# Two attention layers and two feed-forward layers on one core: general path at the end, semaphores cleared as ranges, linear stage with halves in three banks

## The reference

```
x = layernorm(x + linear_attention(x))     # 16 heads of 8: elu(q)+1, elu(k)+1, running sums over time
x = layernorm(x + switch_attention(x))     # 8 heads of 64, 5 experts, 3 chosen per token and head, softmax
x = layernorm(x + rotary_attention(x))     # 16 heads of 8, rotary positions, softmax
x = layernorm(x + ffn(x))                  # only the tokens whose router weight is above the median
```

```
s_t = s_(t-1) + k_t v_t^T ;  z_t = z_(t-1) + k_t
value_t = (q_t^T s_t) / (q_t^T z_t + 1e-6)
```

## Time and profile before

| | us |
|---|---|
| median of three executions | 2010.35 |
| profiled execution, its own time | 2014.0 |
| its span, first to last instruction | 2012.1 |
| linear stage, from the start to the next stage's first instruction | 232.64 |
| expert stage, likewise | 1101.69 |
| rotary stage, likewise | 583.12 |
| depth stage, to the end of the span | 94.65 |

### The profile page before, as it was taken

How to read it: one execution, slowest core, us unless ns; L and a number is a source line. 1 busy time by engine, 2 the same in 40 slices (tenths; PEclk the granted TensorE clock), 3 DMA queues, 4 the chain that set the end, 5 groups by cost and what they waited for, 6 DMA issues and landing times. The chain is left out here.

```text
span 2012.1 us, 25633 instructions
## 1 busy us (share of the span) xinstructions
PE 1750.1 (87%) x8916; PEld 836.6 (42%) x8916; DVE 1149.1 (57%) x1834; ACT 1280.4 (64%) x2456; POOL 953.7 (47%) x565
## 2 busy tenths in 40 slices
PE   7888459999999999999999999636989999998587
PEld 3433245445555455554545544212333333332255
DVE  6988596986668876678766564240303214120267
ACT  1211205766776668766786676606999999999434
POOL 4566306778876788767888678700000000000023
PEclk9988689999999999999999999777999999999879
DMA  2000000000000000000000000013220302110001
GB/s 70 0 1 0 24 20 11 20 21 11 21 20 11 20 11 20 11 20 11 21 20 11 20 11 1 0 44 135 70 80 22 126 22 84 65 41 22 0 15 43
DMA packets 27869, 59.11 MB, mean 29 GB/s; under 512 B 3840, under 2 KB 14800, under 8 KB 27728
## 3 DMA queue, kind: packets, MB, share of 16 engines
q1 hardware_dynamic: 27728, 57.32, 8.9%
HBM read 38.44 MB, written 18.87 MB: 28 GB/s over the span
## 5 line engine op out<-in xcount | busy, mean ns | idle before, releaser
L707 POOL TENSOR_TENSOR b_psum<-b_psum,b_probs 128x1024 f32<-128x1024 f32 x192 | 460.6, 2399 | 173.8 <-ACT b_probs L847 167.1
L2020 ACT ACTIVATE c_probs<-banks 128x1024 f32<-128x1024 f32 x512 | 483.0, 1029 | 67.3 <-PE banks L2072 56.1
L1225 DVE TENSOR_TENSOR b_gated<-banks,b_g 128x480 f32<-128x480 f32 x512 | 314.2, 655 | 229.1 <-PE banks L949 224.2
L847 ACT ACTIVATE b_probs<-banks 128x1024 f32<-128x1024 f32 x256 | 254.1, 1019 | 218.5 <-PE banks L982 217.7
L949 PE MATMUL banks<-b_w,b_xh 128*128 128x480 f32 x1024 | 353.3, 399 | 33.5 <-DVE b_gated L1225 19.4
L1233 DVE TENSOR_REDUCE b_tok<-b_gated 128x192 f32<-128x960 f32 x256 | 281.4, 1138 | 0.5
L982 PE MATMUL banks<-b_qq,b_kk 64*128 64x512 f32 x1024 | 263.7, 625 | 14.7 <-DVE b_gated L1225 10.0
L818 ACT ACTIVATE b_share<-b_o,b_picked 128x64 f32<-128x64 f32 x1080 | 268.6, 338 | 0.0
L1014 PE MATMUL banks<-b_probs,b_tok 128*64 128x512 f32 x1024 | 253.5, 616 | 2.4 <-ACT b_probs L847 2.4
L2087 PE MATMUL banks<-c_probs,c_vg 128*32 128x512 f32 x2048 | 247.7, 601 | 0.3 <-DVE c_acc L2182 0.2
L949 PEld LDWEIGHTS banks<-b_w,b_xh 128*128 128x128 f32 x1024 | 195.0, 190 | 116.5 <-issue 40.3
(11 more groups left out here) (232 smaller groups left out, 1907.6 us busy)
## 6 DMA issues: line engine op xcount, KB each, us to landing
b_raw_w<-in_L_ffn_W SPq DMA_DIRECT2D x32, 480.0 KB, 3.3
c_heads<-c_split SPq DMA_DIRECT2D x24, 512.0 KB
c_keys<-c_heads SPq DMA_DIRECT2D x16, 512.0 KB, 3.7
c_queries<-c_heads SPq DMA_DIRECT2D x16, 512.0 KB, 4.6
c_heads<-c_split SPq DMA_DIRECT2D x8, 384.0 KB
a_xs<-in_L_attn_x SPq DMA_DIRECT2D x4, 512.0 KB, 7.8
out<-d_yo SPq DMA_DIRECT2D x3, 512.0 KB, 3.2
c_heads<-c_split SPq DMA_DIRECT2D x8, 128.0 KB
```

Source lines behind the costliest of these rows:

```text
L707: nc.gpsimd.tensor_tensor(psum[:, par, :], prev, probs[:, i % 4, :], ALU.add).then_inc(psum_rdy, 1)
L847: nc.scalar.activation(probs[:, i % 4, :], score_b[i % 2], ACT.Exp).then_inc(exp_rdy, 1)
L1225: nc.vector.tensor_tensor(shape(gated[:, t % 2, j, :]), shape(proj_b[u % WAYS][:, 0:HALF_W]), g.unsqueeze(2).broadcast_to([P, 3, HD2, E]), ...
L2020: nc.scalar.activation(probs[:, step % 4, c, :, :], unit_b[u % NU], ACT.Exp, scale=float(HD) ** -0.5).then_inc(exp_rdy, 1)
```

## The change

The general paths of the two attention stages, and now also a general copy of the depth stage, stand together in one block at the end (`redo_all`). It reads r1 again, so the fast rotary stage writes into a new buffer, r3, and the depth stage reads it. The two flags are kept apart and joined by a maximum; each engine loads and tests the result once. The expert stage raises its flag ahead of its last norm, and the rotary stage counts and raises its flag ahead of and between its last pieces.

Semaphores are kept in a `Signals` object per stage. They are cleared by GpSimd at the start of the next stage's block, one instruction per run of adjacent numbers, so a stage is followed by one barrier and no clearing block. The depth stage's weights are loaded at the end of the rotary stage's SP program.

In the linear stage a column of v is made and multiplied by k in halves of 512 time steps, in three single banks in rotation. The fourth bank's first element holds the constant 1 that the scan reads, broadcast. `scan` and `qscan` have three buffers.

The diff, cut to its core (re-indented lines of the stages are left out):

```diff
+    def clear(self, eng):
+        numbers = sorted(handle.num for handle in self.handles)
+        first = 0
+        for n in range(1, len(numbers) + 1):
+            if n == len(numbers) or numbers[n] != numbers[n - 1] + 1:
+                eng.sem_clear(range(numbers[first], numbers[n - 1] + 1))
+                first = n
...
 def only_if(eng, flag):
-    return nullcontext() if flag is None else eng.If(eng.value_load(flag[0:1, 0:1], min_val=0, max_val=1))
+    return eng.If(eng.value_load(flag[0:1, 2:3], min_val=0, max_val=1))
...
-def linear_scans(nc, x_dram, out, ps, ident, I):
+def linear_thirds(nc, x_dram, out, ps, ident, I, place, signals):
...
-        ones = sb("ones", [P, T])
-        kv, scan, qscan = sb("kv", [P, 3, T]), sb("scan", [P, 2, T]), sb("qscan", [P, 2, T])
+        kv, scan, qscan = sb("kv", [P, 3, T]), sb("scan", [P, 3, T]), sb("qscan", [P, 3, T])
-        v_b, num_b = [bank2(0), bank2(2)], bank2(4)
+        v_b, one, num_b = [ps[:, i, :] for i in range(3)], ps[:, 3, 0:1], bank2(4)
...
-            nc.gpsimd.memset(ones[:, :], 1.0).then_inc(ones_rdy, 1)
...
-                if j == 2:
+                if j == 3:
                     pool.wait_ge(filled, index["den", b, 0] + 1)
-                elif s >= 2:
-                    done = b * HD + j - 2 if j > 2 else b * HD if j == 1 else b * HD - 1
-                    pool.wait_ge(acc_ps, done)
-                nc.gpsimd.tensor_tensor(qscan[:, s % 2, :], scan[:, s % 2, :], q[:, b % 2, :], ALU.mult).then_inc(qs_rdy, 1)
+                elif s >= 3:
+                    pool.wait_ge(acc_ps, b * HD + (j - 3 if j > 3 else j - 2))
+                nc.gpsimd.tensor_tensor(qscan[:, s % 3, :], scan[:, s % 3, :], q[:, b % 2, :], ALU.mult).then_inc(qs_rdy, 1)
...
-            def value_column(g):
-                if g >= 2:
-                    pe.wait_ge(kv_rdy, g - 1)
-                if m == 0:
-                    pe.wait_ge(*reads(index["turn_x", b, 1]))
-                for s in range(0, T, HALF):
-                    last = nc.tensor.matmul(v_b[g % 2][:, s:s + HALF], wv[:, m, :], xT[:, b % 2, s:s + HALF], start=True, stop=True)
-                last.then_inc(v_ps, 1)
+            def value_half(g, s):
+                b, m, n = g // HD, g % HD, 2 * g + s
+                if n >= 3:
+                    pe.wait_ge(kv_rdy, n - 2)
+                if m == 0:
+                    pe.wait_ge(*reads(index["turn_x", b, s]))
+                nc.tensor.matmul(v_b[n % 3], wv[:, m, :], xT[:, b % 2, s * HALF:(s + 1) * HALF], start=True, stop=True).then_inc(v_ps, 1)
...
             for b in range(B):
                 for j in range(NJ):
-                    if j < HD and b * HD + j + 2 < B * HD:
-                        value_column(b * HD + j + 2)
+                    if j < HD:
+                        value_half(b * HD + j + 1, 1)
+                        value_half(b * HD + j + 2, 0)
                     if j:
                         pe.wait_ge(qs_rdy, b * NJ + j + 1)
...
             def key_value(b, m):
-                nc.vector.scalar_tensor_tensor(kv[:, g % 3, :], v_b[g % 2], bv[:, m:m + 1], k[:, b % 2, :], ALU.add, ALU.mult).then_inc(kv_rdy, 1)
+                for s in range(2):
+                    n, cols = 2 * g + s, slice(s * HALF, (s + 1) * HALF)
+                    dve.wait_ge(v_ps, n + 1)
+                    nc.vector.scalar_tensor_tensor(kv[:, g % 3, cols], v_b[n % 3], bv[:, m:m + 1], k[:, b % 2, cols], ALU.add, ALU.mult).then_inc(kv_rdy, 1)
...
-                nc.vector.tensor_tensor_scan(scan[:, s % 2, :], ones[:, :], added, 0.0, ALU.mult, ALU.add).then_inc(scan_rdy, 1)
+                nc.vector.tensor_tensor_scan(scan[:, s % 3, :], one.broadcast_to([P, T]), added, 0.0, ALU.mult, ALU.add).then_inc(scan_rdy, 1)
...
 (expert stage)
         @block.gpsimd
         def _(pool):
-            with only_if(pool, redo):
+            if past is not None:
+                past.clear(pool)
...
                 for half in range(2):
                     pe.wait_ge(zT_sb, Z_COPIES * (B - 1) + 3 * half + 3)
+                    if half == 0 and not with_max:
+                        turn_counts(nc, pe, judged, good, ident, last_b[2][0:1, 0:P])
                     for c in range(3):
...
                 if not with_max:
                     count_safe(nc, dve, judged, recips[:, :], ok, good)
+                    raise_flag(nc, dve, judged, last_b[2][0:1, 0:P], total, P * B * NH * NT, flag[0:1, 0:1])
                 last_norm(B - 1)
-                if not with_max:
-                    raise_flag(nc, dve, judged, last_b[2][0:1, 0:P], total, P * B * NH * NT, flag)
...
 (rotary stage)
             batches(sp, batch)
+            ahead(sp)
...
             turn(B - 1, NP - 1, z_index(B, 0) - NX)
+            turn_counts(nc, pe, judged, good, ident, unit_b[0][0:1, 0, 0:P])
             for k, (kind, half) in enumerate(Z_PIECES):
                 piece(z_index(B, k) - NX, kind, half, B - 1, B * NP)
-            if True:
-                turn_counts(nc, pe, judged, good, ident, piece_b[0:1, 0:P])
...
             normalize(B - 1, NP - 1)
+            count_safe(nc, dve, judged, recips[:, :], ok[:, :], good)
             for k, (kind, half) in enumerate(Z_PIECES):
                 piece(z_index(B, k) - NX, kind, half, B - 1)
+                if k == 1:
+                    raise_flag(nc, dve, judged, unit_b[0][0:1, 0, 0:P], total, P * B * H * NT, flag[0:1, 1:2])
+                    nc.vector.tensor_tensor(flag[0:1, 2:3], flag[0:1, 0:1], flag[0:1, 1:2], ALU.max).then_inc(judged, 1)
             norm(B - 1)
-            if True:
-                count_safe(nc, dve, judged, recips[:, :], ok[:, :], good)
-                raise_flag(nc, dve, judged, piece_b[0:1, 0:P], total, P * B * H * NT, flag)
...
+def redo_all(nc, r1, r2, out_dram, ps, ident, I, past, flag):
...
+        @block.tensor                      # the other engines likewise; GpSimd clears `past` first
+        def _(pe):
+            with only_if(pe, flag):
+                expert.tensor_body(pe)
+                meet(pe, 1)
+                rotary.tensor_body(pe)
+                meet(pe, 2)
+                depth.tensor_body(pe)
+                meet(pe, 3)
+    with nc.Block() as block:
+        @block.gpsimd
+        def _(pool):
+            signals.clear(pool)
...
+        linear, expert, rotary, depth = (Signals(nc) for _ in range(4))
+        linear_thirds(nc, I["L0_attn_x"], r1, ps, ident, I, nc.Block(), linear)
+        switch_attention(nc, r1, r2, ps, ident, I, nc.Block(), expert, linear, False, flag, "b_")
+            rotary_twos(nc, r2, r3, ps, ident, I, nc.Block(), rotary, expert, lambda sp: weights.load(sp, I), flag, "c_")
+            depth_lead(nc, r3, out_dram, ps, ident, I, nc.Block(), depth, rotary, weights, True, "d_")
+        redo_all(nc, r1, r2, out_dram, ps, ident, I, depth, flag)
```

More of the change, by code:

```diff
@@ new lines, in period @@
+            def period(n, b, h, par, before, ahead, start, has_next, projecting, splitting, slots, norm_last, gates_next):
+                for i in range(1, NT):
+                    add_probs(n, par, i)
+                    if i == 3 and norm_last and h == 6:
+                        inverse_roots(b - 1)
+                    if i == 1 and n >= 2:
+                        add_share(1, n - 2, *((b, h - 2) if h >= 2 else (b - 1, NH - 2 + h)))
+                    if i == 5 and splitting:
+                        low_weights(n + 3, 1 - par)
+                    if i == 7 and not start:
+                        add_share(0, n - 1, *before)
@@ new lines, in batch @@
+            def batch(b, first, last):
+                pool.wait_ge(used, z_index(b, 0))
+                for g in range(NG):
+                    pool.wait_ge(pv_done, ONE + VC * (b * NG + g))
+                    for hh in range(G):
+                        at = (g * G + hh) * HD
+                        nc.gpsimd.tensor_copy(vg[:, g % 2, :, hh, 0:HD], v[:, bass.ds(b * NT, NT), at:at + HD]).then_inc(vg_rdy, 1)
+                    if g == 2:
+                        residual(b)
+            batches(pool, batch)
@@ new lines, in _ @@
+            pe.sem_inc(score_ps, ONE + SC)
+            pe.sem_inc(pv_done, ONE + VC)
+            pe.wait_ge(w_in, W_IN)
+            pe.wait_ge(clear, 1)
+            pe.wait_ge(swapped, 8)
+            for j, src in enumerate((0, 1, 4, 5)):
+                last = nc.tensor.matmul(ps[:, 0, j:j + 1], rows[:, src, :], ones[0:1, 0:1], start=True, stop=True)
+            last.then_inc(bias_ps, 1)
+            for j in range(2):
+                nc.tensor.matmul(ps[:, 1 + j, 0:D], ones[0:1, 0:P], rows[:, 2 + j, :], start=True, stop=True).then_inc(bias_ps, 1)
@@ new lines, in _, with batch @@
+            pe.sem_inc(filled, NZ)
+            def batch(b, first, last):
+                at = pieces(b, first, last)
+                for i in range(BS):
+                    scores(b, i, first, (NZ if first else 0) + sum(j < i for j in at))
+                    if i:
```

(14 more changed lines are left out.)

1864 lines of the change are left out of this document (935 added, 929 removed).

## The result

The kernel before took 2010.88 us (median of 4 runs beside it), the changed one 1979.99 us (1975.5 to 1982.5, 4 runs): ratio 0.984, 95% interval 0.983 to 0.9853. A second group, of 4 runs, gave 0.9852 (0.9837 to 0.9867). The profiled execution took 1978.8 us for a span of 1977.0, where 2012.1 stood.

A forecast was written before the change was run, and what follows sets the result against it. Bound: in the linear stage, two-SBUF-operand scans and GpSimd products exclude each other; between stages nothing computes. Savings 26.0 + 2.0 + 12.1 + 11.1 less 3.45 give 47.8 us off 2010.35: 1962.5 us, range 1949 to 1985.

The forecast's parts named there:

- TensorE's pace: Rival, linear stage: at TensorE's low clock for half the stage, the gain there is 13 us, total 1975.5; chance 0.07.
- Scan with its constant in PSUM: Linear stage: with one SBUF operand the scan no longer excludes GpSimd's product; its step becomes 2.26 us, 0.06 added.
- The lock stays: Rival, linear stage: scan and GpSimd product keep alternating, the stage gains nothing, total 1988.5 us; chance 0.08.
- slower than before: Rival, linear stage: a scan rereading one PSUM cell runs at half rate, 4.56 us, total 2028; chance 0.03.
- Halves: Linear stage: key-value product as two 512-column instructions, about 0.67 us each for one of 1.18; VectorE 1.3 us more per batch.
- Order on TensorE: Linear stage: a half column stands behind the numerator that waits for GpSimd; VectorE waits 3.8 us in a middle batch.
- The ring: Linear stage: scan, GpSimd product, numerator, half column, half key-value product in a cycle, 8.05 us per two steps.
- I assume its clock mostly at the high level: Linear stage: TensorE's clock, 0.87 to 0.97 of the high level before, stays mostly high, as there are fewer gaps.
- Clears and boundaries: Between stages: range clears and one barrier replace single clears and skips; 2.0 us less before expert, 11.8 before rotary, 9.0 before depth.
- Rotary stage: Rotary stage's tail: counting and flag move ahead of the last transposes, 3.1 us less against 2.1 more, 1.0 less.
- Depth stage: Depth stage: weights loaded earlier, so the router product starts 1.1 us sooner; TensorE's clock could shift it 2 us either way.
- The end: After the depth stage: flag load, branch over the general bodies and barrier, 5.65 us against 2.2, so 3.45 more.

## Why the prediction was right, and where its terms were off

The forecast was 1962.5 us in 1949 to 1985; 1979.99 came, inside the range and in the direction given, 17.5 us above the point. By the stages the gain was 12.6 us smaller than laid out (linear 10.9, rotary 5.1, end 1.9, less the 4.2 of the depth stage and the 1.1 of the expert stage that came on top). The other 4.9 are, but for rounding, the distances of the two profiled executions from the medians (2014.0 from 2010.35, 1978.8 from 1979.99), which the forecast took as alike. The likeliest case alone had been put at 1951 to 1975. The result lies outside that, in the stretch that the range held for TensorE's pace, a mechanism that the rows show only in patches; that it fell inside is in part luck. The directions and the main mechanism, a scan that nothing holds, were not. By its own steps:

- *Scan with its constant in PSUM:* right. No lock, 2.28 us each; a PSUM operand costs the scan nothing, where 0.06 was allowed. "The lock stays" and "slower than before" fall.
- *Halves:* right. VectorE's busy time came out at 153.3 us over the four batches; the forecast laid out 155.2 (175.6 less 20.4 of waits). The rival of the slow scan started from 159 instead, which its terms don't give; from 155.2 it comes to 2024 us, not 2028, and nothing hangs on it.
- *Order on TensorE:* the term that was mis-sized. Waits of 20.4 us were laid out over the four batches, 33.4 came (186.7 - 153.3). The ring was seen, but only waits of 0.8 at the second and 1.1 at the eighth column of a middle batch were given to it. In the trace they are at the second, seventh and eighth column, at 1.4 to 1.6 us each, and in the first batch at four columns (9.0 us of waits there for 4.2). In the last batch it took 7.1 us from the last scan to its values, for 5.5. The forecast's ring holds only the numerator and the half column; left out were the next batch's q and k products, which stand between them, 1.7 us at the seventh and eighth column. In the last batch, without them, there is no wait at these two. Putting the half column ahead of both gave 10.2 of the missing 11 us back.
- *"I assume its clock mostly at the high level":* nearly so (0.92 to 0.96); each middle batch has one numerator at the lower level behind TensorE's wait for GpSimd, the last has two. One costs the engine 1.7 us and may be part of the waits above. "TensorE sets the pace" gave 1975.5 and lies closer in number, but its mechanism, a stage at the low level half of the time, isn't what the rows show.
- *Clears and boundaries:* right to 0.1 us each. Ranges are cheap. (The clears between expert and rotary stage, read as 43 and 43, are 41 and 45.) The 0.25 us of the expert stage can't be seen in its spread.
- *Rotary stage:* -1.0 forecast, +4.1 measured. The tail did what was said in direction and half of it in size (19.1 to 18.6 us), and 0.8 came in the stage's first 47 us. Missing was a shift of 0.3 us elsewhere that turns a near miss of two engines into a collision of 3.9 us. What stretches the aggregates from 0.64 to 0.90 us and shortens GpSimd's copies was not isolated; it is there in every kernel with the new linear stage and absent with the old.
- *Depth stage:* -1.1 forecast, -5.3 measured: 1.8 by the load, 3.5 with the clock, above the 2 us left open for it.
- *The end:* +3.45 forecast, +5.3 measured. The branch was right (4.3 us, 4.2 taken); the rest around it, the clears and two barriers, was taken as 1.5 and is some 3. In the changed kernel each engine's next row comes 3.0 to 4.4 us behind the start of its branch, SyncE's too; TensorE's is the longest and hides the others.

## What to carry to other kernels

When an instruction of one engine is put behind another that waits for a third engine, lay out every turn of that ring with all that the engine issues in between, not the first few turns; if the order allows it, issue what the bottleneck waits for first. Look at the memories of a VectorE instruction's inputs beside a GpSimd stream: a constant moved to one PSUM cell was worth 25 us here. Two tensors in SBUF aren't the only form that is held; a scaling with one was too (2360 ns for 340), so look for the stretched row itself. A change moves everything behind it by fractions of a microsecond, so look in the trace for pairs of conflicting instructions that only just miss each other, and put distance between them.

## What was not expected of the hardware

- A scan of 1024 columns takes 2.28 us with its constant in an SBUF tile, an SBUF column or a PSUM cell alike, when nothing holds it.
- The taken branch over a general path costs TensorE 3.5 to 4.6 us in its own row; for SyncE, at the end, the row shows 0.05 us, and its next instruction comes 2.4 to 3.0 us later.
- Clearing a range took at most 0.26 us, against 0.07 from one single clear to the next before.
- The same instructions leave the expert stage between 1086.0 and 1092.4 us long, with TensorE's granted share as the only difference seen.
